# 64-key attentions with a third step of lead, queries and keys in the PSUM bank of the first transposes, and ctx moments and tables moved within the first layer

## What is computed

```python
# L0: 16 heads of 64, relative positions; keys are ctx and x, 128 in all
kv = concat([memory, layer_input], axis=1)
q, k, v = layer_input @ Wq, kv @ Wk, kv @ Wv
r = pe @ Wr
scores = ((q + content_bias) @ k + rel_shift((q + position_bias) @ r)) / sqrt(64)
out = ln(layer_input + softmax(scores) @ v @ Wo);  out = ln(out + relu(out @ W1) @ W2)
# L1: 16 heads of 8, 64 keys, shared 8x8 weights per head, integer masks
sa  = attention(x, x, x, mask1);       out = ln(x + sa)          # "msa"
ca  = attention(ctx, ctx, out, mask2); out = ln(out + ca)        # "ca1"
out = ln(out + relu(out @ W1) @ W2)
# L2: three rounds of a gate from the mean of ctx over its tokens
fused = x + sigmoid(x_proj @ Wg_t + (routing * v_proj) @ Wg_v + bg) * routing * v_proj
# L3: 64 keys, no mask
x = x + mha(ln(x), ln(x))                                        # "sa"
x = x + mha(ln(x), ln(ctx))                                      # "ca"
x = x + mixture_of_experts(ln(x))                                # top 2 of 8
```

## Time and profile before

| | us |
|---|---|
| median of 3 runs | 2027.27 |
| lowest, highest | 2026.01, 2027.56 |
| the profiled execution | 2030.62 |
| its span in the profile | 2029.1 |
| PE, PEld busy | 1658.9, 1291.2 |
| DVE, ACT, POOL busy | 1376.8, 1144.0, 959.4 |
| first layer, from its first step | 37.7 to 636.3 |
| pair 1: msa, then ca1 | 713.2 to 1122.7 |
| pair 2: sa, then ca | 1336 to 1700 |

### The profile page before, as it was taken

The page is one execution under the profiler, slowest core; times in us unless marked ns, Lnnn a source line. Parts: engine busy times, 40 slices in busy tenths (PEclk is TensorE's granted clock), DMA queues, the critical chain, the costliest instruction groups (busy, mean ns, idle before and its releaser), DMA issues. The chain is left out here.

```text
span 2029.1 us, 56439 instructions
## 1 busy us (share of the span) xinstructions
PE 1658.9 (82%) x17626; PEld 1291.2 (64%) x17626; DVE 1376.8 (68%) x4296; ACT 1144.0 (56%) x3299; POOL 959.4 (47%) x1434
## 2 busy tenths in 40 slices
PE   5899999999996879998888765369998885439882
PEld 5788888888884756666666652146666664337771
DVE  2677777777776568787777547867787774328773
ACT  1577777777773345666665322247777773117771
POOL 1434444443433434556666423434444443646773
PEclk9999999999998989999999785779999996559996
DMA  6766666666660032220000000000000000126665
GB/s 184 147 152 151 151 145 143 157 144 150 151 149 25 0 133 96 94 81 16 16 16 13 1 0 1 0 4 0 0 6 11 12 12 11 46 96 199 211 209 157
DMA packets 214507, 166.84 MB, mean 82 GB/s; under 512 B 27344, under 2 KB 188496, under 8 KB 214160
## 3 DMA queue, kind: packets, MB, share of 16 engines
q1 hardware_dynamic: 205840, 142.85, 28.3%
q0 software_dynamic: 8576, 22.88, 3.3%
HBM read 91.92 MB, written 73.76 MB: 82 GB/s over the span
## 5 line engine op out<-in xcount | busy, mean ns | idle before, releaser
L842 POOL TENSOR_TENSOR sb_work<-sb_work,sb_cols 128x512 f32<-128x512 f32 x128 | 134.4, 1050 | 299.2 <-ACT sb_work L1056 191.0
L701 ACT ACTIVATE sb_probs<-sb_probs,sb_work 128x128 f32<-128x128 f32 x512 | 198.7, 407 | 114.4 <-DVE sb_work L626 114.4
L983 DVE TENSOR_REDUCE sb_work<-PS 128x8 f32<-128x512 f32 x256 | 175.1, 684 | 53.1 <-PE PS L883 53.0
L280 POOL TENSOR_SCALAR sb_next_var_eps<-sb_next_moments 128x1 f32<-128x1 f32 (+1 forms) x184 | 43.4, 236 | 321.5 <-DVE sb_next_moments L275 321.3
L1021 ACT ACTIVATE sb_work<-sb_work 128x512 f32<-128x512 f32 x256 | 161.2, 630 | 56.0 <-DVE sb_work L985 55.8
L861 PE MATMUL PS<-sb_ident,sb_work 128*128 128x128 f32 x1024 | 165.2, 285 | 33.6 <-ACT sb_work L1021 28.2
L985 DVE TENSOR_TENSOR sb_work<-PS,sb_work 128x512 f32<-128x512 f32 x256 | 176.9, 691 | 8.8
L861 PEld LDWEIGHTS PS<-sb_ident,sb_work 128*128 128x128 f32 x1024 | 114.7, 143 | 68.5 <-ACT sb_work L1021 55.2
L906 PE MATMUL PS<-sb_v_ones,sb_work 128*64 128x18 f32 x4096 | 144.7, 214 | 1.9 <-ACT sb_work L1027 1.8
L906 PEld LDWEIGHTS PS<-sb_v_ones,sb_work 128*64 128x64 f32 x4096 | 132.2, 139 | 19.6 <-issue 7.3
L1027 ACT ACTIVATE sb_work<-PS 128x512 f32<-128x512 f32 x256 | 139.4, 595 | 4.9 <-PE PS L861 1.7
(11 more groups left out here) (273 smaller groups left out, 4472.7 us busy)
## 6 DMA issues: line engine op xcount, KB each, us to landing
rel_scratch<-sb_work SPq DMA_DIRECT2D x64, 516.0 KB, 7.7
sb_work<-rel_scratch SPq DMA_DIRECT2D x64, 512.0 KB, 6.6
expert_rows<-sb_blank SPq DMA_DIRECT2D x36, 520.0 KB, 2.9
sb_w_up<-expert_halves SPq DMA_DIRECT2D x23, 512.0 KB
sb_w_down<-expert_halves SPq DMA_DIRECT2D x23, 512.0 KB
expert_halves<-sb_e_halves POOLq DMA_DIRECT2D x16, 512.0 KB, 5.8
sb_work<-expert_rows SPq DMA_DIRECT2D x23, 260.0 KB, 3.5
sb_e_raw<-e_W POOLq DMA_DIRECT2D x16, 256.0 KB, 6.8
```

The costliest lines, as they stand in the source:

```text
L701: ins = e.activation(probs[:, j], probs[:, j], ACT.Exp, bias=neg_max[:, j:j + 1], scale=-1.0, accum_out=row_sum[:, j:j + 1])
L842: e.tensor_tensor(k_masked[:, u], k_sb[:, u].rearrange("p (b k) -> p b k", b=2).unsqueeze(2) .to_broadcast([P, 2, 4, S]), col("place").uns ...
L983: e.tensor_reduce(top, mine, AX.X, ALU.max).then_inc(sem("att_max_ready"), 1)
```

## The change

1. *Start of the first layer.* The first meeting and the waits for all parameters go; `ident` is loaded with the first tables. The VO products stand in step n = -3, behind that step's K products, in banks 4 to 7. VectorE copies the relative bias before it splits w_k0. POOL's preparations (`prepare_later`) come at its step n = 2, and the bias rows' products at the end of the first layer.
2. *Moments of ctx.* They leave ca1's steps. In the first layer VectorE adds a reduction between x_hi and x_lo and two pairs of statistics and aggregates on 64 partitions at the end of a step; POOL keeps them. At the start of pair 1 POOL makes all inverse deviations with one power, and SP spreads them with two DMAs.
3. *Attentions.* `head` is tile n+3 and `front` n+2, four steps in a loop body; `att_probs` and `v_ones` have four buffers. Queries and keys go to bank 4, with a semaphore of their own (`att_qk_done`), and each copy signals; the transposes of probabilities wait for those copies. V is made from duplicated halves of yT or cT with two products of 128 columns. The transpose of ctx comes right behind the scores.
4. *ScalarE.* ctx is copied before y and c, k before q, v before the second exponential.

```diff
@@ walk_pair
-        return [pair[t // units] if 0 <= t < 2 * units else None for t in (n + 2, n + 1, n, n - 1)]
+        return [pair[t // units] if 0 <= t < 2 * units else None for t in (n + 3, n + 2, n, n - 1)]
...
-    with e.Fori(1, units // 2 - 1) as k:
-        for u in range(2):
+    with e.Fori(1, units // 4 - 1) as k:
+        for u in range(4):
@@ l0_pool
-            e.wait_ge(sem("params_loaded"), 16 * len(loads))
...
-            meet(e, 0)
...
+                if isinstance(n, int) and n == 2:
+                    prepare_later()
...
+                if has(3):
+                    t = n + 3
+                    wait_alone(e, sem("ctx_moments"), t + 1)
+                    e.tensor_tensor(c_moments[:, :, bass.ds(t, 1)].rearrange("p b a m -> p b (a m)"), c_last,
+                                    zeros[0:S, 0:1].unsqueeze(2).to_broadcast([S, 2, 2]), ALU.add)\
+                        .then_inc(sem("ctx_moments_kept"), 1)
@@ l0_tensor
+                if isinstance(n, int) and n == -3:
+                    e.wait_ge(sem("l0_vo_loaded"), 32)
+                    for g in range(4):
+                        e.wait_ge(sem("l0_rel_kept"), g + 1)
+                        for i in range(4):
+                            h = head_at(4 * g + i)
+                            ins = e.matmul(PS[:, 4 + g, i * P:(i + 1) * P], wvT[:, h], wo0[:, h], start=True, stop=True)
+                        ins.then_inc(sem("l0_table_done"), 1)
@@ l0_vector
                     e.tensor_copy(x_hi0[:, :], transposed).then_inc(sem("l0_kv_kept"), 1)
+                    e.tensor_reduce(pooled[:, bass.ds(2 * t, 2)],
+                                    transposed.rearrange("p (b a k) -> p a b k", b=2, a=2)[:, 0], AX.X, ALU.add)
...
+                if has(3):
+                    t = n + 3
+                    wait_alone(e, sem("ctx_moments_kept"), t)
+                    for b in range(2):
+                        ins = e.bn_stats(c_stats[:, b], kv_in[0:S, (u + 3) % 4, b])
+                    ins.then_inc(sem("ctx_stats"), 1)
+                    wait_alone(e, sem("ctx_stats"), t + 1)
+                    for b in range(2):
+                        ins = e.bn_aggr(c_last[:, b], c_stats[:, b])
+                    ins.then_inc(sem("ctx_moments"), 1)
@@ att_pool
+                e.tensor_tensor(c_norms[:, 1], c_var_eps, half_power[0:S, 0:1].unsqueeze(2).to_broadcast([S, 2, NT]), ALU.pow)\
+                    .then_inc(sem("ctx_moments_kept"), 1)
@@ att_tensor
                 if back:
+                    if front:
+                        e.wait_ge(sem("att_qk_kept"), 2 * n + 6)
                     transpose_probs(n, u, 0)
...
+                if late:
+                    e.wait_ge(sem("att_ctx_ready"), n)
+                    wait_alone(e, sem("att_added"), n - 1)
+                    e.transpose(PS[:, 6, 2 * P:3 * P], att_ctx[:, 1 - u % 2], ident[:, :]).then_inc(sem("att_ctxT_done"), 1)
...
                     e.wait_ge(sem("att_T_kept"), m + 1)
-                    wait(e, sem("att_qk_kept"), m)
+                    wait(e, sem("att_qk_kept"), 2 * m)
+                    if back:
+                        e.wait_ge(sem("att_probsT_kept"), 2 * n + 1)
+                    src = yT if cross is None else cT
+                    e.matmul(PS[:, 4, P:2 * P], wk, src[:, u3, :, 0], start=True, stop=True)
+                    e.matmul(PS[:, 4, 0:P], wq, yT[:, u3, :, 0], start=True, stop=True).then_inc(sem("att_qk_done"), 1)
                     wait(e, sem("att_v_ready"), m)
-                    e.matmul(PS[:, 7, 0:P], wq, yT[:, u], start=True, stop=True)
-                    e.matmul(PS[:, 7, P:2 * P], wk, src[:, u], start=True, stop=True)
                     for b in range(2):
-                        for half in range(2):
-                            ins = e.matmul(PS[S * half:S * half + S, 7, (2 + b) * P:(3 + b) * P],
-                                           src[:, u, S * b:S * b + S], wv, start=True, stop=True)
+                        ins = e.matmul(PS[:, 7, (2 + b) * P:(3 + b) * P], src[:, u3, b], wv, start=True, stop=True)
@@ att_vector
-                if front and front["cross"] == 0:
-                    t = n + 1 - front["i"] * NT
-                    e.tensor_reduce(pooled[:, bass.ds(2 * t, 2)],
-                                    cT[:, v].rearrange("p (b s) -> p b s", b=2), AX.X, ALU.add)
-                    moments_vector(e, "ctx", t + 1, lambda _: c_tok[:, v], c_stats, c_moments, 1)
```

More of the change, by code:

```diff
@@ L390, in l0_pool, with prepare_later @@
             e.memset(zeros[:, :], 0.0)
[L391 to L398, removed]
-            e.tensor_copy(blank[:, :, D:D + 1].bitcast(U32), ids[:, 2 * NT:].unsqueeze(2)).then_inc(sem("blank_ready"), 1)
+            e.wait_ge(sem("l0_table_drained"), 6)
+            def prepare_later():
+                e.wait_ge(sem("params_loaded"), 16 * len(loads))
+                e.tensor_copy(ident_16[:, :], ident[:, :])
+                e.tensor_copy(bv_wide[:, 0], col("sa_bv").to_broadcast([P, P]))
+                e.tensor_copy(bv_wide[:, 1], col("ca_bv").to_broadcast([P, P])).then_inc(sem("bases"), 1)
+                e.tensor_tensor(bases[:, 0], row("ln11_b"), row("ca1_bo"), ALU.add)
+                e.memset(blank[:, :, 0:D], 0.0)
+                e.memset(blank[:, :, D + 1:ROW], 0.0)
+                e.tensor_copy(blank[:, :, D:D + 1].bitcast(U32), ids[:, 2 * NT:].unsqueeze(2)).then_inc(sem("blank_ready"), 1)
             def fetch_expert(k):
@@ L669, in step @@
                 if has(0):
+                    if isinstance(n, int) and n == 0:
+                        e.wait_ge(sem("params_loaded"), 16 * len(loads))
                     e.wait_ge(sem("l0_out_done"), n + 1)
@@ L689, in l0_vector @@
             walk_ahead(e, NT, step)
+            e.wait_ge(sem("bases"), 2)
+            for i, bias in enumerate(("sa_bo", "ca_bo")):
+                e.tensor_tensor(bases[:, 1 + i], PS[:, 2, P * i:P * i + P], row(bias), ALU.add)
         def l0_scalar(e, c):
-            meet(e, 0)
             def step(k, u, has):
@@ L931, in step @@
                     e.wait_ge(sem("att_ctxT_kept"), n)
-                    e.matmul(PS[:, 6, 3 * P:4 * P], att_ctxT[:, 1 - u], w_out[late["name"]][:, :], start=True, stop=True)\
+                    e.matmul(PS[:, 6, 3 * P:4 * P], att_ctxT[:, 1 - u % 2], w_out[late["name"]][:, :], start=True, stop=True)\
                         .then_inc(sem("att_out_done"), 1)
@@ L1028, in step @@
                             .then_inc(sem("att_probsT_kept"), 1)
+                if late:
+                    e.wait_ge(sem("att_ctxT_done"), n)
+                    if head:
+                        e.wait_ge(sem("att_transposed"), n + 4)
+                    wait(e, sem("att_out_done"), n - 2)
+                    e.activation(att_ctxT[:, 1 - u % 2], PS[:, 6, 2 * P:3 * P], ACT.Copy).then_inc(sem("att_ctxT_kept"), 1)
                 if head:
@@ L1070, in step @@
                     ins.then_inc(sem("att_v_ready"), 1)
+                if front:
+                    exponent(1)
             walk_pair(e, pair, NT, step)
```

240 lines of the change are left out of this document (121 added, 119 removed).

## The result

The changed kernel takes **1999.15 us** (median of 4 runs, 1994.92 to 2001.38) against 2026.64; the ratio is 0.986, 95% interval 0.9842 to 0.9877. It is faster by 27.5 us, clear of the spread of the runs, where 59 were forecast: inside the range, but less than half of the forecast gain. The span of the profiled execution is 1999.8 us against 2029.1, 29.3 less.

A forecast was written before the change was run, and what follows sets the result against it. TensorE was taken to bound the first layer, loops of hand-offs between engines the attentions. Terms -15 + 12 + 4 + 1 + 9 - 36 - 34 = -59 gave 1971.6 us on the profile's basis, 1968 for the median; range 1940 to 2005.

The forecast's parts named there:

- Loops of four steps cost more: Attentions: each of 24 remaining loop ends costs 1.0 us in place of .50, 12 us more, 1980 us; chance 3%.
- Start: First layer's start: without the wait for all parameters, the scratch write lands at 42 instead of 57.4 us, -15.
- Wait for x_lo: First layer: ctx moments on VectorE delay x_lo, so TensorE waits .4 us in each of 29 steps, +12.
- Power: Start of pair 1: POOL's inverse deviations of ctx take 10.6 us ahead of the first mask, partly hidden, +4.
- Attention steps: Both pairs: steps fall to 5.6 us in msa, 5.55 ca1, 5.0 sa, 5.15 ca; -36 and -34.
- the two fillings at +4.5: Both pairs: the pipeline starts three tiles ahead, one more filling step of about 4.5 us per pair, +9.
- the bank-4 rival: Attentions: transposes of probabilities wait for the q and k copies sharing bank 4; slower, 2101 us; chance 7%.
- V's form: Attentions: V from two 128-column loads in place of four of 64; counted at nothing, at most .1 us a step.
- half the gain: Attentions: TensorE's in-order stream holds the steps, so half of the 70 us is lost, 2003 us; chance 20%.
- The first layer doesn't stall: First layer: VectorE works ahead by the added .93 us, so the +12 falls away, 1956 us; chance 13%.

The follow-up runs named there:

- the run with 95 memsets: The changed kernel with 95 one-column memsets on VectorE ahead of its first-layer loop, the loop's work unchanged: 1970.63 us, ratio 0.9726 to the kernel before.
- moments_in_ca1: The changed kernel with the sum over ctx, its moments and POOL's power per tile back in ca1's steps: 1972.51 us, ratio 0.9722 to the kernel before.

## Why the prediction was wrong, point by point

**The step that failed** is the one by which the rival "Loops of four steps cost more" was set aside. The rival had the right mechanism, a loop's return that costs more, and set it in the attentions, at .5 us, with 3%; in the sum, the first layer's part was the +12 alone, and its five returns stood at nothing. Its reason against was that the first layer "runs four steps a body at 17.85 with no late step". That row was true of a program in which VectorE's body began at 295. The change puts the same loop at 328, and its five returns each cost about 7.3 us: 589.7 us from first to last L535 with holes, 553.3 without them in the run with 95 memsets, 36.4 in all. The sum counted what stands in the moved instructions and nothing for what their number does to the code behind them. The Trainium skill's Runtime: NRT & Kernel Launch, section Instruction fetch mechanics, was cited for the wrong loop; its rule, that a taken branch beyond the fetched window stalls, fits these runs. Its pages of 256 instructions don't: with a window of two of them a body of 270 that is free at both 295 and 423 would be free at 352 and 392 too, and no error of my count mends that. Such a window leaves one costly stretch in every 256 places, and the costly shifts of 57 and 97 are parted from that of 219 by free ones on both sides, 128 on the one and 0 and 256 on the other.

The run with 95 memsets is the change without the holes: its span is 1969.1 us, 60.0 less than before, against 59 forecast. Of the layer's 36.4 us, 30.7 reach its end; the rest is lost in small differences of the later stages. That 60.0 meets 59 so closely is in part luck, as the terms show:

- *Start*, -15: right, -13.9. The write landed by 43.46, and with the wait put back 10.2 us of it went.
- *Wait for x_lo*, +12: right in place and size. The steps rose from 17.85 to 18.16, and from 543.7 to 553.3 us over the layer without holes; the first interval before had held 2 us of the start, and .4 at each of the five returns is in it. Moving the statistics removed it whole. A row of the changed kernel shows TensorE waiting within L535:

```profile
613.31 2.74 PE L535 MATMUL PS<-sb_probsT,sb_kv_in 128*128 128x512 f32 x6
616.29 1.10 PE L535 MATMUL PS<-sb_probsT,sb_kv_in 128*128 128x512 f32 x2 [0.25 <-DVE sb_x_lo L674]
```

- *Power*, 10.6 us long, +4: right. It took 10.54, and pair 1's first mask came 9.88 us behind the first transpose of y (759.49 less 749.61), where it came 5.94 behind it with the power per tile again (706.46 less 700.52 in `moments_in_ca1`):

```profile
746.72 10.54 POOL L858 TENSOR_TENSOR sb_c_norms<-sb_c_var_eps,sb_half_power 64x64 f32<-64x64 f32 x1
```

- *Attention steps*, -36 and -34: -43.8 and -27.8. Of the two fillings at +4.5, pair 1's is in the +10.0 of the table and pair 2's doesn't show (+.4). In full turns of the loop msa's steps average 5.57 (5.6 forecast), ca1's 5.39 (5.55), sa's 4.9 (5.0), ca's 5.7, where 5.15 stood. In ca TensorE waits for two copies of ScalarE's in each step:

```profile
1593.78 0.46 PE L964 MATMUL PS<-sb_work,sb_w_ca 128*128 128x128 f32 x2 [0.40 <-ACT sb_work L1087]
1595.35 1.09 PE L899 MATMUL PS<-sb_ident,sb_work 128*128 128x128 f32 x8 [0.21 <-ACT sb_work L1100]
```

  The second is the bank-4 rival's wait, real but .2 us in a step that was still shorter than before. And in ca a return of the loop costs .7 to 1.8 us over two steps, 1.3 on average, where the sum had .5: there the loop rival was right in its own place, for some 4 us.
- *V's form*, counted at nothing: wrong by 21 us in the pairs, hidden in the attentions' sum. With four products, as that sum had it, the pairs gave 50.6 us (728.1 less 677.5) and not 70: that -43.8 and -27.8 come to 71.6 is luck: a part counted at nothing made up for hand-offs that gave some 20 us less than forecast. The Trainium skill's TensorE: Matmul & The Clock Gate, section on LDWEIGHTS, has the load time go with the columns, by which both forms cost the same; these rows say .67 and .90.
- *Rivals*: "half the gain" gave 2003, near the measured time, by luck: its 35 us less was to come from the attentions, and these gave 71.6 of 70. Its reason, TensorE's own stream, isn't refuted: shortening it by v's form was worth 21 us. "The first layer doesn't stall" was wrong; it did by .31.

## What to carry to other kernels

When an edit adds instructions ahead of a long loop or in it, the place of the loop in its engine's program is part of the price: read the first row behind the branch on each engine for idle time put down to issue, and the packets of the instruction queues. Shift the loop by a few dozen cheap instructions before blaming the work. And put work where a row shows its engine idle: the same four operations cost 9 us at the end of a step and nothing ahead of a wait of 2.4 us.

## What the runs showed of the hardware

A return of a loop of 270 or 294 instructions on VectorE left it idle for 5.1 to 9.1 us or for .3 to .4, by the loop's place in the program. Places 128 and 256 instructions behind a free one were free, those 57, 97 and 219 behind it weren't, and each costly return came with about five more packets on an instruction queue, where the free ones had none. What reaches TensorE was less when VectorE came to its branch 1.1 us earlier: 4.4 us for 6.1 at one return. Four products with 64 columns of weights took .23 us more than two with 128, for the same weights and results, in the step shown.
